# A fused decoder layer on one core: order of the prelude and of the first step

## What is computed

```python
pos_cos, pos_sin = cos(pp), sin(pp)                        # pp = pos_phases[:L]
pos_values = x @ Wpv + bpv
pos_mem_cos, pos_mem_sin = cumsum(pos_cos * pos_values), cumsum(pos_sin * pos_values)
pos_ret = (pos_cos * pos_mem_cos + pos_sin * pos_mem_sin) / sqrtD
key_ph = tanh(x @ Wk + bk) * pi
kv_values = x @ Wkv + bkv
gh = gelu(concat([x, x_shifted]) @ Wg1 + bg1)
value_gates = sigmoid(gh @ Wg2 + bg2)
kv_mem_cos = cumsum(shift(cos(key_ph)) * kv_values * value_gates)   # kv_mem_sin alike
kv_ret = (key_cos * kv_mem_cos + key_sin * kv_mem_sin) / (sqrt(gate_cumsum) * sqrtD)
bw = softmax(gelu(x @ Wb1 + bb1) @ Wb2 + bb2)
blended = bw[..., 0:1] * pos_ret + bw[..., 1:2] * kv_ret
return x + layernorm(blended, ln_g, ln_b) @ Wo + bo        # then x + this, layernorm
```

## Time and profile before

| | us |
|---|---|
| median of 3 runs (2293.61 to 2300.7) | 2298.87 |
| the profiled execution | 2301.51 |
| its span, on which all rows stand | 2299.7 |
| TensorE busy | 2005.8 (87%) |
| VectorE busy | 1765.3 (77%) |
| ScalarE busy | 1550.1 (67%) |
| first matmul begins | 16.36 |
| `mix_out(0)`, the first work of step 1, begins | 72.78 |

### The profile page before, as it was taken

How to read it: one execution, slowest core, us unless ns; L and a number is a source line. 1 busy time by engine, 2 the same in 40 slices (tenths; PEclk the granted TensorE clock), 3 DMA queues, 4 the chain that set the end, 5 groups by cost and what they waited for, 6 DMA issues and landing times. The chain is left out here.

```text
span 2299.7 us, 43580 instructions
## 1 busy us (share of the span) xinstructions
PE 2005.8 (87%) x10638; PEld 1059.2 (46%) x10638; DVE 1765.3 (77%) x3666; ACT 1550.1 (67%) x4346; POOL 707.9 (31%) x919
## 2 busy tenths in 40 slices
PE   6988988499999999999999998886645999999993
PEld 2454555133222232222332221113535999999993
DVE  4968875399999999999999999995653555555554
ACT  3455555399999999999999999994211333333334
POOL 0001100044444444444444441111772222333331
PEclk9989989699999999999999999997767999999997
DMA  4111103746676675775766755635732222222224
GB/s 149 42 41 69 55 23 128 148 76 104 129 130 110 131 102 124 120 122 128 112 118 115 135 105 68 97 47 177 241 123 59 37 37 37 37 37 37 37 37 156
DMA packets 130113, 217.32 MB, mean 94 GB/s; under 512 B 20290, under 2 KB 100802, under 8 KB 129938
## 3 DMA queue, kind: packets, MB, share of 16 engines
q1 hardware_dynamic: 103072, 152.25, 35.7%
q0 software_dynamic: 25440, 63.46, 10.0%
q10 hardware_dynamic: 1554, 1.05, 0.2%
HBM read 137.97 MB, written 78.72 MB: 94 GB/s over the span
## 5 line engine op out<-in xcount | busy, mean ns | idle before, releaser
L1349 ACT ACTIVATE probs<-psum,neg_max 128x512 f32<-128x512 f32 (+1 forms) x1664 | 1112.3, 742 | 45.9 <-DVE neg_max L1257 44.7
L1257 DVE TENSOR_REDUCE neg_max<-psum 128x1 f32<-128x512 f32 (+1 forms) x1664 | 1025.4, 676 | 18.7 <-PE psum L1194 15.3
L1194 PE MATMUL psum<-qst,kst 96*128 96x512 bf16 (+1 forms) x1664 | 530.7, 391 | 100.3 <-ACT probs L1349 61.5
L1162 PE MATMUL psum<-probs,v_scaled 128*32 128x512 f32 (+1 forms) x3328 | 450.1, 614 | 9.2 <-DVE attn L1271 9.2
L1194 PEld LDWEIGHTS psum<-qst,kst 96*128 96x128 bf16 (+1 forms) x1664 | 130.3, 98 | 688.7 <-ACT probs L1349 641.2
L1349 ACT ACTIVATION_READ_ACCUMULATOR probs<-psum,neg_max 128x1 f32 (+1 forms) x1664 | 436.1, 262 | 0.0
L1845 ACT ACTIVATE hid<-psum,b 128x128 f32<-128x128 f32 x568 | 162.5, 369 | 393.2 <-PE psum L1818 392.6
L1321 POOL TENSOR_TENSOR v_scaled<-vst,inv 128x64 f32<-128x64 f32 (+1 forms) x416 | 121.6, 292 | 687.8 <-DVE inv L1225 687.8
L1879 POOL DMA_INDIRECT sums_all<-y_out,dest x71 | 154.4, 2175 | 381.2 <-DVE y_out L1924 375.4
L1818 PE MATMUL psum<-xst,w 128*128 128x128 f32 x2272 | 266.6, 276 | 0.0
L1818 PEld LDWEIGHTS psum<-xst,w 128*128 128x128 f32 x2272 | 260.8, 193 | 0.1
(11 more groups left out here) (222 smaller groups left out, 2105.8 us busy)
## 6 DMA issues: line engine op xcount, KB each, us to landing
kst<-k_parts SPq DMA_DIRECT2D x384, 112.0 KB, 6.5
k_parts<-k_out POOLq DMA_DIRECT2D x52, 336.0 KB, 3.1
w_all<-in_W SPq DMA_DIRECT2D x16, 1024.0 KB
ct<-in_ctxT SPq DMA_DIRECT2D x16, 896.0 KB, 4.7
vst<-v_all SPq DMA_DIRECT2D x64, 224.0 KB, 9.1
qst<-q_parts SPq DMA_DIRECT2D x192, 64.0 KB, 5.9
v_all<-v_out POOLq DMA_DIRECT2D x13, 896.0 KB, 4.3
rows_in<-xs SPq DMA_DIRECT2D x71, 129.0 KB, 2.0
```

Of the source, the lines that this page charges most:

```text
L1162: last = pe.matmul(psum[j * PAD:(j + 1) * PAD, 6, :], v_scaled[0:r, pb, j, :], probs[0:r, pb, j, :], start=t == 0, stop=t == ST - 1)
L1194: pe.matmul(psum[0:r, 2 * sbuf + i, :], kst[:, h, j, t * P:t * P + r], qst[:, h, j, :], start=True, stop=True).then_inc(scores_ready, 1)
L1257: v.tensor_reduce(neg_max[0:r, sbuf, i:i + 1], psum[0:r, 2 * sbuf + i], AX_X, ALU.min) \
L1349: act.activation(probs[0:r, pb, j, :], psum[0:r, 2 * sbuf + i, :], ACT.Exp, bias=neg_max[0:r, sbuf, i:i + 1], scale=-1.0, accum_out=sums[0 ...
```

## The change

Four things are moved, and nothing is added to or taken from what is computed.

1. **Loads.** `weights` now holds `cols`, `xt` of element 0, `wpv` and `wk`, in this order and first on SP's queue. The others (`wg1`, `wb1`, `wkv`, `wo`, `wq`) follow on a semaphore of their own, `more_loaded`. `xin` of element 0, which only `xbo` reads, comes behind them.
2. **Position tables.** VectorE reduces the positions first, before it waits for any weight. ACT loads the sine table at once, makes `pos_sin` and `pos_cos`, loads the gelu table, and only then waits for weights.
3. **TensorE.** `wpv` is projected first, then `wk`, then (after `more_loaded`) `wg1` and `wb1`. The wait for `wo_ready` in front of `blend_weights(0, 0)` is gone; `keys(1)` waits for it instead, since the mean of `wo_c` now lies in psum bank 0, which `keys` writes.
4. **Output weights.** VectorE scales `wo_c` in step 0 behind the position scans (`scale_wo`) and centres it in front of the gated values (`centre_wo`).

```diff
             weights = [
                 (cols[:], a["cols"]),
+                (xt[:, 0, :, 1:L + 1], a["xT"][0]),
+                (wpv[:], a["Wpv"].rearrange("(c p) d -> p c d", p=P)),
                 (wk[:], a["Wk"].rearrange("(c p) d -> p c d", p=P)),
+            ]
+            more_weights = [
...
-                    load(0, 0)
+                    sp.sem_inc(xt_loaded[0], 16)
                     for tile, src in weights:
                         sp.dma_start(tile, src).then_inc(weights_loaded, 16)
+                    for tile, src in more_weights:
+                        sp.dma_start(tile, src).then_inc(more_loaded, 16)
+                    sp.dma_start(xin[:, 0].rearrange("p t d -> p (t d)"), a["x"][0]).then_inc(xt_loaded[0], 16)
...
-                        if not (isinstance(b, int) and b == 0):
-                            wait(pe, q_split, PARTS * (b - 1))
+                        if isinstance(b, int) and b == 1:
+                            pe.wait_ge(wo_ready, 1)
+                        else:
+                            pe.wait_ge(q_split, PARTS * (b - 1))
                         project(0, wk, now(h), C).then_inc(kz_ready, 1)
...
-                    pe.wait_ge(xt_loaded[0], 32)
+                    project(5, wpv, now(0), C).then_inc(pv_ready, 1)
                     project(0, wk, now(0), C).then_inc(kz_ready, 1)
+                    pe.wait_ge(more_loaded, 16 * len(more_weights))
                     project(2, wg1, now(0), 2 * C).then_inc(gh_ready, 1)
                     blend(0, 0)
-                    project(5, wpv, now(0), C).then_inc(pv_ready, 1)
-
-                    pe.wait_ge(wo_g_ready, 1)
+                    pe.wait_ge(phase_ready, 1)
+                    pe.wait_ge(derived_ready, 1)
+                    pe.wait_ge(wo_scaled, 1)
...
                     gates(0, 0)
-                    pe.wait_ge(wo_ready, 1)
                     blend_weights(0, 0)
...
+                    act.preload_act_table_set("trig_and_small")
+                    act.wait_ge(consts_made, 1)
+                    act.wait_ge(pos_ready, 1)
+                    act.activation(pos_sin[:], pos[:], ACT.Sin)
+                    act.activation(pos_cos[:], turns[:], ACT.Sin, bias=half_pi[:], scale=-1.0).then_inc(trig_ready, 1)
+                    act.preload_act_table_set("gelu_and_others")
                     act.wait_ge(weights_loaded, 16 * len(weights))
...
+                    def scale_wo():
+                        v.wait_ge(more_loaded, 16 * len(more_weights))
+                        for k in range(C):
+                            last = v.tensor_scalar(wo_c[:, k, :], wo[:, k, :], col(LNG + k), None, ALU.mult)
+                        last.then_inc(wo_scaled, 1)
...
+                        if not end:
+                            scale_wo()
...
+                        if not end:
+                            centre_wo()
                         if mix:
                             v.wait_ge(kv_ready, c + 1)
```

More of the change, by code:

```diff
@@ L250, in decoder_layer @@
             xt_loaded = (sem("xt_loaded0"), sem("xt_loaded1"))
-            weights_loaded, pos_loaded = sem("weights_loaded"), sem("pos_loaded")
+            weights_loaded, more_loaded, pos_loaded = sem("weights_loaded"), sem("more_loaded"), sem("pos_loaded")
             (kz_ready, gh_ready, bh_ready, gate_z_ready, pv_ready, bw_z_ready, kv_ready, mix_out_ready, mix_stats_ready,
@@ L849, in _ @@
                 def _(v):
+                    v.wait_ge(pos_loaded, 16)
+                    v.tensor_scalar(turns[:], pos[:], 1.0 / TWO_PI, ROUND, ALU.mult, ALU.add).then_inc(dve_pos, 1)
+                    v.wait_ge(dve_pos, 1)
+                    v.tensor_scalar(turns[:], turns[:], -ROUND, None, ALU.add).then_inc(dve_pos, 1)
+                    v.wait_ge(dve_pos, 2)
+                    v.scalar_tensor_tensor(pos[:], turns[:], -TWO_PI_HI, pos[:], ALU.mult, ALU.add).then_inc(dve_pos, 1)
+                    v.wait_ge(dve_pos, 3)
+                    v.scalar_tensor_tensor(pos[:], turns[:], TWO_PI_HI - TWO_PI, pos[:], ALU.mult, ALU.add) \
+                        .then_inc(dve_pos, 1)
+                    v.wait_ge(dve_pos, 4)
+                    v.tensor_scalar(pos[:], pos[:], -PI_DOWN, PI_DOWN, ALU.max, ALU.min).then_inc(dve_pos, 1)
+                    v.wait_ge(dve_pos, 5)
+                    v.scalar_tensor_tensor(turns[:], pos[:], -1.0, pos[:], ALU.mult, ALU.max).then_inc(pos_ready, 1)
                     v.wait_ge(weights_loaded, 16 * len(weights))
@@ L879, in _ @@
-                    v.wait_ge(dve_pos, 5)
-                    v.tensor_scalar(pos[:], pos[:], -PI_DOWN, PI_DOWN, ALU.max, ALU.min).then_inc(dve_pos, 1)
-                    v.wait_ge(dve_pos, 6)
-                    v.scalar_tensor_tensor(turns[:], pos[:], -1.0, pos[:], ALU.mult, ALU.max).then_inc(pos_ready, 1)
-                    v.wait_ge(wo_mean_ready, 1)
-                    v.wait_ge(consts_loaded, N_CONSTS)
-                    for k in range(C):
-                        v.tensor_tensor(wo_c[:, k, :], wo_c[:, k, :], psum[:, 7, 0:D], ALU.subtract)
@@ L889, in _ @@
-                    v.tensor_tensor(bo_half[:], rows[:, BO, :], psum[:, 7, D:2 * D], ALU.add).then_inc(wo_ready, 1)
-                    v.wait_ge(wo_ready, 1)
-                    v.tensor_scalar(bo_half[:], bo_half[:], 0.5, None, ALU.mult).then_inc(wo_ready, 1)
-                    v.wait_ge(trig_ready, 1)
+                    v.wait_ge(trig_ready, 1)
+                    def scale_wo():
[3 more added lines that the diff above has]
+                        last.then_inc(wo_scaled, 1)
@@ new lines, in centre_wo @@
+                    def centre_wo():
+                        v.wait_ge(wo_mean_ready, 1)
+                        v.wait_ge(consts_loaded, N_CONSTS)
+                        for k in range(C):
+                            v.tensor_tensor(wo_c[:, k, :], wo_c[:, k, :], psum[:, 0, 0:D], ALU.subtract)
+                        v.tensor_tensor(bo_half[:], rows[:, BO, :], psum[:, 0, D:2 * D], ALU.add).then_inc(wo_ready, 1)
+                        v.wait_ge(wo_ready, 1)
+                        v.tensor_scalar(bo_half[:], bo_half[:], 0.5, None, ALU.mult).then_inc(wo_ready, 1)
@@ L964, in step @@
                             last.then_inc(moments_ready, 1)
-                        if not end or mix:
-                            pass
+                        if not end:
+                            scale_wo()
                         if mix:
```

30 lines of the change are left out of this document (6 added, 24 removed).

## The result

| | before | after |
|---|---|---|
| median, 5 runs each (us) | 2298.6 (2292.61 to 2300.7) | 2282.03 (2281.25 to 2284.18) |
| ratio, with 95% interval | | 0.9938 [0.9921, 0.9955] |
| profiled execution (us) | 2301.51 | 2282.03 |
| first matmul | 16.36 | 11.30 |
| gated values of step 0 | 51.79 | 39.16 |

A forecast was written before the change was run, and what follows sets the result against it. First stage bound by TensorE's late start, idle time and slow passes: 7.1 + 5.2 + 0.3 + 3.1 = 15.7, cut to 15.4 us because VectorE ends later; 2298.87 - 15.4 = 2283.5 us, range 2276 to 2293.

The forecast's parts named there:

- Term 1: TensorE's first product starts at 9.3 instead of 16.36 us, a gain of 7.1 us, bounds 5.6 and 7.9.
- three signs of being wrong: `wk` landing after 11; L1006 beginning after 39; first stage ending under 8 us sooner although `mix_out(0)` is at 57.
- The covers of the new waits: TensorE's waits `more_loaded`, `wo_scaled` and `phase_ready` before the gates cost nothing; the narrowest cover is the cosine's, 2.3 us.
- Term 2: TensorE's idle time before `wg1` of step 0 disappears: 5.2 us, with some 0.3 more from the blend weights.
- Term 3: `wg1` of step 0, without idle time in front, takes 7.03 instead of 10.11 us: 3.1 us, other bound zero.
- `xbo`: GpSimd's `xbo` beside VectorE's gated values in step 0: loss taken as 0, likely at most 0.7, at worst 2.1 us.
- The later steps: Long and short steps after step 0 may be dealt anew: plus or minus 4 us; by the skill's rule, spread, not shift.
- A: Rival: only the start gains, gated values stay late and TensorE idles as before; gain 7.1, 2291.8 us; chance 0.07.
- B: Rival: split loads share engines and the first four tensors land at 14 or so; gain 10.7, 2288.2 us; chance 0.06.
- C: Rival: three short later steps become long; gain 8.2, 2290.7 us, or 2292.5 with a late start; chance 0.07.
- D: Rival: the gain is made up for later, at the hand-over to cross attention or in it; about 2298.9 us; chance 0.04.
- E: Rival: TensorE starts at 9.3 but stays at 1.2 GHz; 9 us slower, 2308, decided from 35 passes on; chance 0.02.

The follow-up runs named there:

- e5: Changed kernel with ScalarE issuing its nine constants behind the position sines instead of right behind the position table; median 2278.67 us, ratio to the kernel before 0.9932.
- e4: Changed kernel with `wpv` projected fourth again, behind `wb1`; 2295.0 us in one run, against the changed kernel's median of 2278.36 on this chip.
- e9: Kernel before with six additional matmuls, results unused, filling TensorE's idle time in step 0; ratio to the kernel before 1.0011.
- e3: Changed kernel with the two position sines back at the end of ScalarE's prelude and `wo_c` scaled in the prelude; ratio to the kernel before 0.9989.
- e2: Changed kernel with only the loads put back in the old order under one semaphore; ratio to the kernel before 0.9968.
- e1: Kernel before with only the loads split in two groups and reordered; ratio to the kernel before 0.9975.

## Why the prediction was right

**Term 1, the start, was mis-sized:** 5.1 us and not 7.1, a little outside its bounds (5.6 to 7.9). Two of the three signs of being wrong that the prediction named came, both by this: `wk` landed after 11 (11.3), and L1006 began later than 39 (39.16). The step that failed is "ACT's queue runs beside it as before", and with it "exactly 1,036 KB": equal bytes, but in other rows, beside a queue with which packets are shared. The trace of before had what was needed, the packets of both queues up to 9.3 us. I looked only at landings. e5 shows the size: without the constants on ACT's queue the start is 7.7.

**The covers of the new waits held.** `more_loaded` did not stop TensorE at 20.69. The cosine ended at 13.0 (forecast 13.2) and the products began with `wpv` at 17.54. `wo_c` was scaled at 25.3, asked for at 29.28. e4 shows what it costs when the cover of `wo_scaled` is gone: 11 us.

**Term 2, the idle time,** was right in mechanism and size. From the gates to `wg1` TensorE took 42.39 - 31.01 = 11.4 us, and 53.25 - 36.30 = 17.0 before: 5.6 less, for 5.2 + 0.3 forecast. Counted from the start, L1006 came at 39.16 - 11.30 = 27.9, forecast 28.2, and `wg1` without a wait 1.8 us behind the end of L1006. The steps from `mix_out(0)` back to the start are 47.8 for 48.1 forecast, so the late start explains the whole miss there: 59.1 for 57.4.

**Term 3, the slow passes:** 3.1 us was right as a term of TensorE's sum (7.04 for 10.11), and e9 shows that it is due to the idle time. It also shows that it isn't a gain by itself: with `wg1` fast, TensorE waited for VectorE, whose 19.8 us from the gated values on had not moved, and `mix_out(0)` came only 1.3 us earlier than in the first profile. It counted here only because the gated values came earlier by as much. Taking the later of two engines (15.4) and not TensorE's list alone (15.7) decided nothing: they ended together, VectorE at 58.96 (57.73 + 1.23) and TensorE's blend weights at 58.99.

**`xbo`** lay beside L1006 from 39.16 to 39.85 and cost nothing: L1006 took 1.41, and the products 3.61. With the stretched products of e3 (4.67) the rule cited for it is borne out on both sides: products of two SBUF operands are slowed, L1006 with one from PSUM is not.

**The later steps** were a spread and no shift, as the second reading had it. Its size, plus or minus 4, fits the spread as a whole (290.9 to 297.3, half of it 3.2), but it was laid around 297.3, the longest sum on record; the changed kernel's four sums are all under it, by 2.0 to 5.1.

**Rivals.** A (the rest doesn't gain) is excluded by e2, B by the start at 11.3 and by e1. C needs three long steps more than before, seven; the changed kernel's profiles have two or three of over 42. D is excluded by the first scores, 18.7 us earlier, the end, 19.5, and the 1925 to 1930 us behind the last `mix_out` in every profile before and after. E would have needed 35 slow passes; the first product had about six (6.12 for 3.60, at 0.44 each). That rests on their length alone, as it does in the prediction: the granted clock reads 1.00 in that stretch.

Two small sums of the prediction are off without consequence: C with a late start gives 2290.7 + 1.5 = 2292.2, not 2292.5, and the bounds named give a lowest forecast of 2278.7, not 2277.

The time fell where it was forecast partly by luck, from two errors that nearly cancel: 1.7 us less at `mix_out(0)`, and in the medians (16.6) some 3 more than the 13.7 of the profiles. What that surplus is stays open; the ratio's 14.3 us (10 to 18) agrees with 13.7 without it.

## What to carry to other kernels

A prologue is a chain like any other: ask of each engine which single input its first useful instruction needs, and put the small operation on which the longest list hangs (here two sines, worth 10 of 14 us) in front of all that merely could be done first. Parts of such a reordering can carry each other, so undo them one at a time before one is dropped. Loads in another queue are not free for the first group: count their packets, and issue constants in small rows when the first group is in. Here that brought the first product 3.5 us forward, though six runs could not show a gain in time from it. And read a gain or a loss of a few us in the steps from several profiles, never from one.

## What was not expected of the hardware

The nine constants, 0.53 MB in 1,210 packets, held the first group back by 3.5 us, about twice what their bytes would cost at the 0.3 MB per us of this stretch. And filling TensorE's idle time with 5.3 us of matmuls kept its clock at 2.4 GHz there, but it was at 1.2 GHz for part of `mix_out(0)`, 18 us later (5.38 us for 3.70), and the kernel became 2.5 us slower, not faster. Nor does the clock need an idle stretch to fall: in the changed kernel it fell in `wkv` of step 1 behind 3.5 us in which TensorE was busy with products of one column.
